# Retention in 64-token chunks: one stretch of quarter products per slot in a fused attention and FFN block

## The reference

```python
q1 = (x @ Wq).reshape(B, N, H, HEAD_QK)
k1 = (x @ Wk).reshape(B, N, H, HEAD_QK)
q1, k1 = apply_rotary(q1, k1)
...
def step(S, qkv):            # over chunks of 64 tokens
    qb, kb, vb = qkv
    attn = jnp.einsum('bhid,bhjd->bhij', qb, kb) * D[None]
    o_intra = jnp.einsum('bhij,bhjd->bhid', attn, vb)
    o_inter = jnp.einsum('bhid,bhde->bhie', qb * cross_q, S)
    S_new = gC * S + jnp.einsum('bhjd,bhje->bhde', kb * cross_k, vb)
    return (S_new, o_intra + o_inter)
...
o = rmsnorm(o, gn_weight)
g = jax.nn.silu(x @ Wg)
o = o.reshape(B, N, VALUE_DIM) * g
return o @ Wo
...
x = _layernorm(x + _L0_attn_ref(...), axis=-1)
x = _layernorm(x + _L0_ffn_ref(...), axis=-1)   # (silu(x@wg) * (x@wu)) @ wd, 256 -> 768 -> 256
```

## Time and profile before

| | |
|---|---|
| three executions | 425.12, 426.88, 427.09 us; median 426.88 us |
| span of the profiled execution | 423.9 us, first to last instruction |
| its own device time | not listed apart from the three; the span is 1.2 to 3.2 us under them |
| PE busy | 418.1 us, 4311 matmuls |
| PEld / DVE / ACT / POOL busy | 396.8 / 312.1 / 259.0 / 188.1 us |
| PE's clock | full throughout |

### The profile page before, as it was taken

How to read it: one execution, slowest core, us unless ns; L and a number is a source line. 1 busy time by engine, 2 the same in 40 slices (tenths; PEclk the granted TensorE clock), 3 DMA queues, 4 the chain that set the end, 5 groups by cost and what they waited for, 6 DMA issues and landing times.

```text
span 423.9 us, 12406 instructions
## 1 busy us (share of the span) xinstructions
PE 418.1 (99%) x4311; PEld 396.8 (94%) x4311; DVE 312.1 (74%) x907; ACT 259.0 (61%) x796; POOL 188.1 (44%) x330
## 2 busy tenths in 40 slices
PE   8999999999999999999999999999999999999995
PEld 7899999999999999999999999999999999999995
DVE  4999677678676778766777666777766777667785
ACT  6568755577566566566566566565666565565552
POOL 2522343445544344444354444354534354444465
PEclk9999999999999999999999999999999999999999
DMA  8931010201111011110001111011110010100002
GB/s 275 376 120 52 0 53 1 65 2 39 39 40 39 2 40 39 39 37 17 27 31 37 37 37 37 0 37 37 37 37 12 1 40 15 39 14 2 15 27 65
DMA packets 14327, 19.66 MB, mean 46 GB/s; under 512 B 1488, under 2 KB 9808, under 8 KB 14288
## 3 DMA queue, kind: packets, MB, share of 16 engines
q1 hardware_dynamic: 14144, 19.08, 13.8%
q10 hardware_dynamic: 144, 0.07, 0.1%
HBM read 14.94 MB, written 4.19 MB: 45 GB/s over the span
## 4 chain that ended last, share of the span: by engine, by line
PE 97%; DVE 1%; issue 0%; POOL 0%; ACT 0%; POOLq 0%; ACTq 0%; DVEq 0%
PE b_rows L463 29%; PE b_ffn L463 20%; PE b_rows L481 13%; PE b_rows L477 8%; PE b_head L639 7%; PE b_head L609 4%; PE b_turn L673 3%; PE b_head L605 3%; PE b_ffn L628 3%; PE b_turn L491 2%; PE b_state L658 2%; PE b_state L745 1%; DVE wf_int L1367 1%; PE b_rows L524 0%; PE b_ffn L658 0%
## 5 line engine op out<-in xcount | busy, mean ns | idle before, releaser
L1710 POOL TENSOR_TENSOR h_lo<-wf_int,h_hi 128x256 fp32r<-128x256 f32 x96 | 70.9, 740 | 97.3 <-ACT h_hi L1005 97.0
L463 PE MATMUL b_ffn<-x1T_hi,wf_hi 128*128 128x256 f32 x384 | 92.6, 278 | 0.1
L463 PE MATMUL b_ffn<-x1T_lo,wf_hi 128*128 128x256 f32 x384 | 92.1, 277 | 0.0
L463 PEld LDWEIGHTS b_ffn<-x1T_hi,wf_hi 128*128 128x128 f32 x384 | 72.2, 188 | 0.7 <-DVE wf_int L1344 0.5
L463 PEld LDWEIGHTS b_ffn<-x1T_lo,wf_hi 128*128 128x128 f32 x384 | 72.2, 188 | 0.0
L980 ACT ACTIVATE sq<-b_head 128x128 f32<-128x128 f32 x124 | 34.4, 277 | 50.5 <-PE b_head L639 47.5
L1005 ACT CAST h_hi<-wf_int 128x256 fp32r<-128x256 f32 x96 | 38.8, 404 | 40.6 <-DVE wf_int L1344 39.9
L1728 POOL TENSOR_TENSOR ve<-mv,eps 128x1 f32<-128x1 f32 x63 | 13.7, 217 | 87.3 <-DVE mv L1455 71.0
L481 PE MATMUL b_rows<-wp_hi,xT_lo 128*128 128x256 f32 x198 | 50.0, 277 | 0.0
L1344 DVE TENSOR_TENSOR wf_int<-b_ffn,wf_int 128x256 f32<-128x256 f32 x96 | 40.4, 421 | 11.8 <-ACT wf_int L994 9.0
L1446 DVE TENSOR_TENSOR z<-b_rows,x_sb 128x256 f32<-128x256 f32 x32 | 13.6, 425 | 44.7 <-PE b_rows L463 44.7
(11 more groups left out here) (158 smaller groups left out, 1227.4 us busy)
## 6 DMA issues: line engine op xcount, KB each, us to landing
xT_raw<-in_xT SPq DMA_DIRECT2D x16, 256.0 KB, 2.7
x_sb<-in_x SPq DMA_DIRECT2D x16, 256.0 KB, 2.7
out<-wf_int SPq DMA_DIRECT2D x30, 128.0 KB, 1.7
wf_int<-in_w_ffn SPq DMA_DIRECT2D x6, 384.0 KB, 6.3
wf_int<-in_w_proj SPq DMA_DIRECT2D x6, 256.0 KB, 4.2
rope_sb<-in_rope SPq DMA_DIRECT2D x4, 256.0 KB, 5.7
rope_q<-in_rope_by_row SPq DMA_DIRECT2D x2, 512.0 KB, 8.8
wo_raw<-in_w_o SPq DMA_DIRECT2D x1, 512.0 KB, 6.8
```

The costliest lines, as they stand in the source:

```text
L463: mm = pe.matmul(dst, a, b, start=(i == 0 and j == 0 and not begun), stop=(i == n - 1 and j == len(passes) - 1 and not more), skip_group_c ...
L1710: pool.tensor_tensor(h_lo[:, ring, hb], h_full[:, u], h_hi[:, ring, hb].bitcast(F32), ALU.subtract).then_inc(h_split[j], 1)
```

## The change

From slot 9 on (`PACKED`) all engines follow a new order, `packed_slot`, and tiles 8 to 30 (`chunked`) are retained as two chunks of 64 tokens instead of one of 128.

- The scores are made within each chunk only: 8 quarter products with 64 columns instead of 128. `mask` works on half the columns.
- The second chunk's queries recall from `state_mid`, the state after the first chunk; the first chunk's from `states`. Recall is 8 quarter products as before; for the first tile of a sequence it is the 4 of the second chunk. The last tile of a sequence, which needed no update before, makes the 4 of its first chunk.
- Retain is 8 quarter products of 128 columns instead of 4 full ones. So that a row half of the array and a column half never meet another row half in the same bank, odd heads' two chunks trade places in the output (`out_rows`); the gate is written with the same exchange (`gate_v`, three ACT instructions), and `turn_y` undoes it as it writes.
- PE does recall(m), scores(n), update(n), retain(m) in one stretch, for n = s-1 and m = s-2, so retain comes one slot later; it waits on `scores_done` of the stretch itself. `y`, `turn_y` and Wo come one slot later too, at the places that `packed_slot` gives.
- V and the gate are projected in 256-column halves alone (before: their first two or three passes in 512). ACT's copy `keep_x1` is gone: `norm_1` writes to alternating buffers. The hardware loop is gone, all slots are written out. The order of `drain` is new.

```diff
+PACKED = NATURAL + 1
+CHUNKED = PACKED - 1
...
+        def chunked(n):
+
+            return CHUNKED <= n < NT - 1
...
@@ -257,11 +275,48 @@
 
         def scores_of(n, h):
 
-            return head_bank(n, h % 2)[:, (h // 2) * P:(h // 2 + 1) * P]
+            w = CHUNK if chunked(n) else P
+            return head_bank(n, h % 2)[:, (h // 2) * w:(h // 2 + 1) * w]
...
+        def out_rows(h, a):
+
+            return half(a + h)
+
+        def update_of(n, a):
+
+            return b_state[:, 0:256] if a == 0 else x1_bank(*at(n, 1)[::2])[:, 256:512]
...
+            def heads_ready(s):
+
+                n, m = s - 1, s - 2
+                pe.wait_ge(qkT_kept, n + 1)
+                pe.wait_ge(q_rotated, s - 8 if n % 2 else s - 7)
+                pe.wait_ge(v_copied, n + 1)
+                pe.wait_ge(masked, m + 1)
+                if m >= CHUNKED:
+                    pe.wait_ge(y_ready, m)
+                    pe.wait_ge(mid_kept, m - CHUNKED + 1)
+                else:
+                    pe.wait_ge(state_kept, states_to(m // TS, m % TS))
+                if s < NT:
+                    pe.wait_ge(h_ready[1], s - FFN_LAG)
+
+            def queries(n, h, a):
+
+                at_a = (n % 2) * P + a * CHUNK
+                return qT[half(h), n // 2 % 2, h // 2, at_a:at_a + CHUNK]
+
+            def recall(m):
+
+                for a in range(2):
+                    if a == 0 and m % TS == 0:
+                        continue
+                    kept = states[:, m % 2] if a == 0 else state_mid
+                    for h in range(H):
+                        mm = pe.matmul(o_of(m, h)[out_rows(h, a)], queries(m, h, a), kept[half(h), h // 2],
+                                       start=h < 2, stop=False, skip_group_check=True)
+                return mm
+
+            def retain_chunks(m):
+
+                for h in range(H):
+                    for a in range(2):
+                        mm = pe.matmul(o_of(m, h)[out_rows(h, a)], attn[half(a), h, 0:CHUNK],
+                                       v_sb[half(a), m % 2, h * DV:(h + 1) * DV],
+                                       start=False, stop=True, skip_group_check=True)
+                mm.then_inc(o_done, 1)
+
+            def heads(s):
+
+                n, m = s - 1, s - 2
+                if m >= CHUNKED:
+                    recall(m)
+                for h in range(H):
+                    for a in range(2):
+                        opened = m >= CHUNKED and (m % TS > 0 or (a + h) % 2 == 1)
+                        mm = pe.matmul(scores_of(n, h)[half(a)], qkT[half(h), 2 + h // 2, half(a)], queries(n, h, a),
+                                       start=h < 2 and not opened, stop=True, skip_group_check=True)
+                mm.then_inc(scores_done, 1)
+                for c in range(H // 2):
+                    for a in range(2 if n % TS < TS - 1 else 1):
+                        for h in (2 * c, 2 * c + 1):
+                            mm = pe.matmul(update_of(n, a)[half(h), c * DV:(c + 1) * DV],
+                                           qk[half(a), n % 2, 256 + h * DK:256 + (h + 1) * DK],
+                                           v_sb[half(a), n % 2, h * DV:(h + 1) * DV],
+                                           start=c == 0, stop=True, skip_group_check=True)
+                mm.then_inc(update_done, 1)
+                if m >= CHUNKED:
+                    pe.wait_ge(scores_done, n + 1)
+                    retain_chunks(m)
...
+            def packed_slot(s, wide):
+
+                q, t = s // TS, s % TS
+                ready = lambda: heads_ready(s)
+                down(*at(s - 7, DOWN_LAG), wide, free=(g_gated, s) if s == PACKED else (v_copied, s))
+                if s > PACKED:
+                    gate_up_block(*at(s, -1), 0, wide)
+                gate_up_block(*at(s, -1), 1, wide)
+                if s > PACKED:
+                    turn_y(*at(s - 3, 2))
+                keys_and_queries(s, q, t)
+                gate_up_block(*at(s, -1), 2, wide, ready if s == PACKED else None)
+                if s > PACKED:
+                    attention_out(*at(s - 3, 2), last_waits=ready)
+                heads(s)
+                project(s, q, t, 1, v_done)
+                project(s, q, t, 2, g_done)
+                turn_x1(s, q, t)
+                turn_qk(s, q, t)
 
             def drain(wide):
...
+                down(*at(NT - 7, DOWN_LAG), wide, (0,), free=(g_gated, NT), more=True)
+                down(*at(NT - 7, DOWN_LAG), wide, (2,), begun=True, more=True)
+                gate_up_block(*at(NT - 1, 0), 1, wide)
+                turn_y(*at(NT - 3, 2))
+                gate_up_block(*at(NT - 1, 0), 2, wide)
+                heads_ready(NT)
+                last_recalls()
+                attention_out(*at(NT - 3, 2), free=(v_copied, NT))
+                gate_up_block(*at(NT - 1, 0), 0, wide)
+                down(*at(NT - 6, DOWN_LAG), wide, (2,), free=(z1_ready, NT - 2), more=True)
+                down(*at(NT - 6, DOWN_LAG), wide, (1,), begun=True, more=True)
+                last_retain()
+                down(*at(NT - 7, DOWN_LAG), wide, (1,), begun=True)
+                turn_x1(*at(NT - 3, X1T_LAG))
+                turn_y(*at(NT - 2, 2))
+                down(*at(NT - 6, DOWN_LAG), wide, (0,), begun=True)
+                gate_up_block(*at(NT, 0), 0, wide)
+                attention_out(*at(NT - 2, 2), free=(z2_ready, NT - 6))
+                turn_y(*at(NT - 1, 2))
+                gate_up_block(*at(NT + 1, 0), 0, wide)
+                gate_up_block(*at(NT, 0), 1, wide)
...
+                    by_head = lambda ap: ap.rearrange("p (c a n) -> p a c n", a=2, n=DV)
+                    src, dst = by_head(g_bank(s, t)[:]), by_head(g_sb[:, t])
+                    act.activation(dst[:, 0], src[:, 0], ACT.Silu)
+                    for a in range(2):
+                        last = act.activation(dst[half(1 - a), 1], src[half(a), 1], ACT.Silu)
+                    last.then_inc(g_gated, 1)
...
+            def packed_slot(s):
+
+                q, t = s // TS, s % TS
+                b, tb = s - 1, (s - 1) % TS
+                if s == PACKED:
+                    mean_squares(*at(s - 2, 1))
+                else:
+                    split_x1T(*at(s - 4, X1T_LAG))
+                    gate_v(*at(s, -1))
+                if exists(s + 3):
+                    split_xT(*at(s, 3))
+                keep_qk(s, q, t)
+                if s > PACKED:
+                    gate(b, tb, 0)
+                gate(b, tb, 1)
+                if s > PACKED:
+                    split_y(*at(s - 3, 2))
+                split_h(b, tb, 0)
+                split_h(b, tb, 1)
+                gate(b, tb, 2)
+                turn_q(s, q, t, 0)
+                turn_q(s, q, t, 1)
+                split_h(b, tb, 2)
+                if s > PACKED:
+                    mean_squares(*at(s - 2, 1))
+                copy_v(s, q, t)
 
             def early_slot(s, q, t):
                 prev = (s - 1, *back(q, t, 1))
...
+                    if chunked(n):
+                        if n == CHUNKED:
+                            dve.wait_ge(chunk_filled, 1)
+                        for a in range(2):
+                            last = dve.tensor_tensor(by_half[:, a, :, 0:CHUNK],
+                                                     b_head[a][:, 0:2 * CHUNK].rearrange("p (c n) -> p c n", c=2),
+                                                     causal_chunk[:].unsqueeze(1).broadcast_to((P, 2, CHUNK)), ALU.mult)
+                        last.then_inc(masked, 1)
+                        return
...
+            def add_first_half(n):
+
+                old, new = (x.rearrange("p c n -> p (c n)") for x in (states[:, n % 2], state_mid[:]))
+                dve.wait_ge(update_done, n - CHUNKED + 1)
+                if n % TS == 0:
+                    last = dve.tensor_copy(new, update_of(n, 0))
+                else:
+                    last = dve.tensor_tensor(new, update_of(n, 0), old, ALU.add)
+                last.then_inc(mid_kept, 1)
+
+            def add_second_half(n):
+
+                if n % TS < TS - 1:
+                    old, new = (x.rearrange("p c n -> p (c n)") for x in (state_mid[:], states[:, (n + 1) % 2]))
+                    dve.wait_ge(mid_kept, n - CHUNKED + 1)
+                    dve.tensor_tensor(new, update_of(n, 1), old, ALU.add).then_inc(next_kept, 1)
...
+            def packed_slot(s):
+
+                q, t = s // TS, s % TS
+                b, tb = s - 1, (s - 1) % TS
+                if s > PACKED:
+                    split_x1T(*at(s - 4, X1T_LAG))
+                norm_2(*at(s - 8, DOWN_LAG + 1))
+                if s == PACKED:
+                    finish_first_q()
+                else:
+                    gated_output(*at(s - 3, 1))
+                residual_2(*at(s - 7, DOWN_LAG))
+                if s > PACKED:
+                    hidden(b, tb, 0)
+                hidden(b, tb, 1)
+                if s > PACKED:
```

(16 more changed lines are left out.)

648 lines of the change are left out of this document (375 added, 273 removed).

## The result

The changed kernel takes 423.48 us (median of 4 executions, 423.20 to 423.66) against 426.25 (425.12 to 427.09) for the kernel before beside it: ratio 0.9929, interval 0.9905 to 0.9953. It is faster, by 2.8 us where 10.6 were forecast, and 423.48 lies above the range of 414.0 to 422.0. The profiled executions differ by 2.4 us in their span (423.9 and 421.5) and by 3.05 at the last matmul (419.03 and 415.98). By the starts of the scores the 3.05 divide so: the scores of tile 8 start 1.14 earlier (100.73 for 101.87; slot 9 has less work in the new order, which comes later), from there to tile 9's 0.19 is gained, in the 21 slots from tile 9's scores to tile 30's 5.89 (261.85 for 267.74), and the drain takes 4.16 more.

A forecast was written before the change was run, and what follows sets the result against it. The sum of PE's matmul times, 12.77 us per slot, was taken as the bound. Terms -10.3 - 5.1 + 2.6 + 2.2 - 1.0 + 1.0 = -10.6 took 426.9 to 416.3 us; range 414.0 to 422.0, 8 in 10.

The forecast's parts named there:

- Retain, scores, V and gate: Per tile, retain falls from 0.89 to 0.44 us, scores from 0.44 to 0.22; V and gate save about 0.045 per slot.
- First and last tiles: In a sequence's first tile recall gains four products, in its last tile update does: +2.6 and +2.2 us.
- Recall's order: 17 tiles ask for diagonal quarters twice, then the others twice; taken as 0, as a rival +3.7 us, chance 0.15.
- Retain's bank: Rival: both row halves writing into one bank make retain run two at a time; +10.3 us, 426.6; chance 0.06.
- (a): Retain waits for its own stretch's scores, 0.28 us, covered by 0.44 of update; cost 0, else 0.3 per slot.
- (b): `turn_y` stands 3.2 us into the slot; DVE's work up to `y` takes 2.4 with semaphores; 0.8 to spare.
- (c): Retain's end to `y` took 4.15 us; now 3.2 to the slot's end and 3.2 more; nothing late.
- So these 0.3 us stay: Going into quarters (about 0.09 plus 0.05 us) and coming out (about as much) costs the same per slot before and after.
- A 256-column pass takes 0.113: Price in us of one 256-column pass on PE; twelve passes of V's projection take 1.36.
- Slots 9 and 10, and the tail: Slots starting the new order with less work in them, and the tail: +0.6 us, guessed between 0 and 1.5.
- Drain: +0.4: Between last retain and its `turn_y` PE has 3.83 us of work against the chain's 4.15: +0.4 us.
- rival 3: The wait in the stretch is not covered: 0.3 x 23 = +6.9 us, 423.2; chance 0.07.

The follow-up runs named there:

- wide_scores: Changed kernel with each chunk's scores computed twice side by side (128 columns, second copy unused): 427.73 us, 4.4 more than the changed kernel.
- full_retain: Changed kernel with retain as 4 products on the full array in place of 8 quarter products: 433.66 us, some 10 more than the changed kernel.
- keys_early: Changed kernel with the product of keys and queries one block earlier, behind the first FFN block: 440.44 us, some 17 slower than the changed kernel.
- the fastest kernel: Changed kernel with gate ahead of V in slot 9, queries before keys from slot 10, tile 31's residual and moments before norm_2 in drain: 421.91 us.

## Why the prediction was wrong

**The bound** was read rightly: PE's sum decides in every steady slot. wide_scores and full_retain put work back into PE, and all of it reached the end.

**Retain, scores, V and gate:** right. 0.44, 0.23 (forecast 0.22) and 2.72 for V and gate (was 2.77, switches aside). **First and last tiles:** right; their stretches take 1.69 and 1.71 (213.42 to 215.11, 238.33 to 240.04), as long as an inner tile's 1.72, because the two quarters in use carry as much as there. **Recall's order:** cost 0, as taken. The Trainium skill (TensorE: Matmul & The Clock Gate, Part 3, "The mechanism") has matmuls start strictly in program order. The trace disagrees: the rows of 225.85 and 225.88 show later ones of a free quarter starting ahead. **Retain's bank:** two row halves write to different halves of one bank at full pace, 16 matmuls in 0.44. The Trainium skill (TensorEngine Tiling (Array Packing), Gotcha 1) has it otherwise, and the trace disagrees. **Waits (a), (b), (c)** in steady slots: 0, right; keys_early showed a wait that I had not looked at, Wo's for `y`, with 0.8 us to spare. One reading was off without a cost: V's first pass stands at 210.57 in the earlier trace rows, not at 210.65, for it starts 0.03 behind the last transpose and is longer by as much.

**"So these 0.3 us stay"** (entry and exit of the stretch) is a step that failed. The change moves what stands behind the quarters: transposes before, a 256-column pass after. 0.23 instead of 0.165 each time, 1.5 us. I could have seen it: the earlier trace rows has the exit onto transposes, not onto a pass. full_retain adds that full-array fp32 products don't make it cheaper: 0.12 and 0.10 (231.25 and the product behind it).

**"A 256-column pass takes 0.113"**, used for every pass of the changed kernel, is the largest miss: 2.6 us of 118-ns passes. No row shown announced it, though the trace of the kernel before has 125 of them, a block behind the queries' product in one slot of four, 0.65 us in all. Shown: they belong to the program and come in nearly every slot at the same instructions; they don't come from written-out code, DMA, the place of the waits, DVE's rotation or the granted clock; in 20 of 22 slots they start behind the queries' product where a 256-column pass follows it. Not shown: the cause. It stays open, and neither the weight loads nor the other engines' work at that time, DVE's rotation aside, was tested by itself. Every edit of the order that freed one group of them made another slow: 703 to 873 in the same 276 us, and 587 at the least, in the fastest kernel.

**Slots 9 and 10, and the tail: +0.6, a guess.** Slot 9 alone cost 1.2 to 1.4, of which gate ahead of V gave back 0.64 (12.83 to 12.19 us from tile 8's scores to tile 9's). I had costed which work is missing there, but not what that work covered (ACT's copies of the queries).

**Drain: +0.4** was computed for one chain, `y` to `turn_y`, which had no wait (and 4.15 less 3.83 is 0.32). 2.6 it was, at seven other places. The gap that I looked for is that of the old order; a new order in which PE has little other work has its own.

The account: -10.6; scores 0.4 (0.20 to 0.21 a tile for 0.22), 118-ns passes 2.6, exit 1.5, slot 9 and tail 0.6 to 0.8 over the guess, drain 2.2 over the 0.4: -3.1 to -3.3, and -3.05 at the last matmul. The 0.6 at the very end, scatter for the most part, brings the span to -2.4. The entries are each read from a trace, slot 9 and the work of chunks are shown by experiments too. The 118-ns passes and the exit are measured, but no experiment took them away; of the drain's 2.6 only 0.3 to 0.4 was undone.

No rival was right either, though rival 3's time (423.2) is near the result: its mechanism, a wait ahead of retain, isn't there. A time that fits doesn't show a cause.
